# One-core delta-rule attention and routed feed-forward: separate semaphore instructions against counts that ride on the work

## What is computed

```python
# attention: q, k, v, gate, beta by projections of layernorm(x); 16 heads of 32
def step(S, inp):                      # one token, all heads
    k_t, q_t, v_t, beta_t, a_t = inp
    S = S * a_t[..., None, None]
    kv_mem = jnp.einsum('bhd,bhde->bhe', k_t, S)
    delta = (v_t - kv_mem) * beta_t
    S = S + k_t[..., :, None] * delta[..., None, :]
    return S, jnp.einsum('bhd,bhde->bhe', q_t, S)
x = x + layernorm(rmsnorm(ys) * silu(gate) @ Wo.T + bo)
# feed-forward: one of 16 columns per token (top-1 of similarity + sigmoid(gelu gate)),
# y = weight * gelu(x @ W_col + b_col) @ proj + proj_b + x
x = x + layernorm(layernorm(y) * ln_g + ln_b)
```

## Time and profile before

| | us |
|---|---|
| runs (3) | 4015.16, 4022.54, 4012.38 |
| median | 4015.16 |
| profiled execution, its own time | 4013.22 |
| its span, first to last instruction | 4011.4 |
| PE busy, DVE busy | 3183.0, 2954.6 |
| ACT busy, POOL busy | 1356.0, 1903.3 |
| mean granted clock of PE | 0.887 of full |

### The profile page before, as it was taken

The page is one execution under the profiler, slowest core; times in us unless marked ns, Lnnn a source line. Parts: engine busy times, 40 slices in busy tenths (PEclk is TensorE's granted clock), DMA queues, the critical chain, the costliest instruction groups (busy, mean ns, idle before and its releaser), DMA issues. The chain is left out here.

```text
span 4011.4 us, 150558 instructions
## 1 busy us (share of the span) xinstructions
PE 3183.0 (79%) x59368; PEld 2416.1 (60%) x59368; DVE 2954.6 (74%) x12372; ACT 1356.0 (34%) x2440; POOL 1903.3 (47%) x2903
## 2 busy tenths in 40 slices
PE   5788888888888888888888888888888888536664
PEld 4666666666666666666666666666666666424442
DVE  1577877777777777778777777777778777746786
ACT  2233333333333333333333333333333333124553
POOL 0544455444444445444554444544454445414776
PEclk9898999988888898988889988988899889768997
DMA  3654444555544445544455554454555444518995
GB/s 107 119 105 93 97 95 96 103 107 107 97 97 98 95 97 107 107 96 88 93 99 107 107 105 96 96 98 92 104 107 105 94 93 94 104 61 228 231 228 119
DMA packets 400616, 438.62 MB, mean 109 GB/s; under 512 B 34624, under 2 KB 338368, under 8 KB 399440
## 3 DMA queue, kind: packets, MB, share of 16 engines
q1 hardware_dynamic: 383312, 395.67, 47.9%
q0 software_dynamic: 16640, 33.71, 3.8%
HBM read 357.55 MB, written 75.93 MB: 108 GB/s over the span
## 5 line engine op out<-in xcount | busy, mean ns | idle before, releaser
L406 PE MATMUL work<-xT,w_sb 128*128 128x256 f32 x5120 | 1352.6, 416 | 19.1 <-PEq L397 9.5
L1003 POOL TENSOR_TENSOR pairs<-pairs,beta 128x240 f32<-128x240 f32 (+14 forms) x1920 | 851.6, 482 | 891.7 <-POOLq L999 891.7
L406 PEld LDWEIGHTS work<-xT,w_sb 128*128 128x128 f32 x5120 | 1017.9, 206 | 213.0 <-issue 60.3
L1216 DVE TENSOR_TENSOR uk<-uk,Ut 128x120 f32<-128x120 f32 (+14 forms) x3840 | 710.4, 227 | 0.0
L1213 DVE TENSOR_TENSOR Ut<-pairs,uk 128x120 f32<-128x120 f32 (+14 forms) x3840 | 693.9, 218 | 11.4 <-DVEq L1204 6.2
L514 PE MATMUL work<-wo_sb,ctxT 128*128 128x512 f32 x512 | 255.0, 644 | 48.9 <-PEq L397 46.7
L1016 POOL TENSOR_TENSOR kd<-kd,dec 128x512 f32<-128x512 f32 x64 | 68.9, 1076 | 440.0 <-POOLq L1014 434.3
L770 ACT ACTIVATE qraw<-work 128x512 f32<-128x512 f32 x128 | 75.8, 592 | 477.5 <-ACTq L769 477.5
L450 PE MATMUL uk<-kqd,S 32*32 32x32 f32 x8192 | 129.1, 206 | 125.9 <-issue 104.9
L1228 DVE TENSOR_TENSOR S<-Sd,su 128x512 f32<-128x512 f32 x64 | 44.0, 687 | 232.8 <-DVEq L1227 232.8
L1034 POOL TENSOR_TENSOR xfw<-xfw,pb_sb 128x1024 f32<-128x1024 f32 x32 | 75.2, 2351 | 293.7 <-POOLq L1033 293.7
(11 more groups left out here) (211 smaller groups left out, 5872.5 us busy)
## 6 DMA issues: line engine op xcount, KB each, us to landing
pairs<-pair_rows SPq DMA_DIRECT2D x512, 480.0 KB, 8.2
w_sb<-in_w_cols SPq DMA_DIRECT2D x80, 256.0 KB
w_sb<-in_proj_w SPq DMA_DIRECT2D x80, 256.0 KB
pairs<-xs_rows SPq DMA_DIRECT2D x70, 258.0 KB
xt<-in_x SPq DMA_DIRECT2D x66, 256.0 KB
pair_rows<-Ak SPq DMA_DIRECT2D x64, 256.0 KB, 2.6
x<-in_x SPq DMA_DIRECT2D x64, 256.0 KB, 11.7
out<-x SPq DMA_DIRECT2D x64, 256.0 KB, 3.3
```

The source lines that it names most:

```text
L406: mm = pe.matmul(w[:, half * BT:(half + 1) * BT], w_sb[:, f, j * D + hg * P:j * D + (hg + 1) * P], xT[:, f, :], start=(f == 0), stop=(f == ...
L1003: ins = nc.gpsimd.tensor_tensor(a, a, beta[:, :, t:t + WID[t0]], ALU.mult)
L1216: link(v.tensor_tensor(uk[:, g, at + 1:at + 1 + n], uk[:, g, at + 1:at + 1 + n], Ut[:, g, 0:n], ALU.subtract), behind=1)
```

## The change

Signals of the main phase become counts that are never taken down. `Chain.__call__` gets a `signal`: the instruction then raises that signal itself instead of the step semaphore, and the engine does not wait for it unless `hold` says so. `take` waits until a count has reached the sum of all that this reader has taken so far, less `free` for resources that start out free. As nothing is taken down, one count serves several readers: `S_ready` now serves PE and POOL, `kq_ready` PE, POOL and ACT; `kqd_ready`, `A_ready`, `eg_ready`, `xf_ready` also stand for "free" signals that are gone. The bank signals `work_free` are gone too: `into` waits for the count that the bank's last reader raises anyway (`READ_BY`). A wait directly ahead of an instruction rides on it; a second wait for the same instruction is a semaphore instruction of its own. SP's `store` no longer waits for the landing; `load_residual` waits for the store before. The values, shapes and tiles stay.

```diff
+READ_BY = dict(xT="xT_ready", qk="q_sq_ready", ss="ss_read", alpha="alpha_read", rms="rms_read", G="eg_ready", wo="wo_read",
+               rank="rank_read", gate="gate_used", beta="beta_ready", v="v_read", xfT="xfT_ready", hid="h_ready",
+               logits="logits_read")
...
-    def __call__(self, ins, behind=0):
-
+    def __call__(self, ins, signal=None, behind=0, hold=False):
+
+        if signal:
+            self.sent[signal] += 1
+            ins.then_inc(self.s[signal], 1)
+            if hold:
+                self.hold(signal)
+            return
         self.n += 1
         ins.then_inc(self.sem, 1)
         self.eng.wait_ge(self.sem, self.n - behind)
+
+    def hold(self, signal):
+        self.eng.wait_ge(self.s[signal], self.sent[signal])
...
+        seen, sent = Counter(), Counter()
+
+        def take(eng, name, n=1, free=0, use=""):
+
+            seen[eng, name, use] += n
+            if seen[eng, name, use] > free:
+                eng.wait_ge(s[name], seen[eng, name, use] - free)
...
             def load_tokens(i):
-                sp.wait_ge(s["xt_free"], 1)
-                sp.sem_inc(s["xt_free"], -1)
+                take(sp, "eg_ready", 2, free=2)
...
             def load_residual(i):
-                sp.wait_ge(s["x1_free"], 1)
-                sp.sem_inc(s["x1_free"], -1)
+                take(sp, "xf_ready", TB, free=TB)
+                take(sp, "store_done", 16 * BL, free=16 * BL)
...
             def store(i):
...
-                sp.wait_ge(s["store_done"], 16 * BL)
-                sp.sem_inc(s["store_done"], -(16 * BL))
...
             def into(*use):
 
-                pe.wait_ge(bank_free(*use), 1)
-                pe.sem_inc(bank_free(*use), -1)
+                before = holder.get(BANK[use])
+                if before:
+                    pe.wait_ge(s[before[0]], before[1])
+                uses[use[0]] += HID // P if use[0] == "hid" else 1
+                holder[BANK[use]] = READ_BY[use[0]], uses[use[0]]
                 return bank(*use)
...
             def change_state(c, half):
                 if not half:
-                    pe.wait_ge(s["delT_ready"], 1)
-                    pe.sem_inc(s["delT_ready"], -1)
-                    pe.wait_ge(s["kd_ready"], 1)
-                    pe.sem_inc(s["kd_ready"], -1)
+                    take(pe, "delT_ready")
+                    take(pe, "kd_ready")
...
             def copy_and_square(n):
 
-                act.wait_ge(s["qraw_free"], 1)
-                act.sem_inc(s["qraw_free"], -1)
-                act.wait_ge(s["qk_full"], 1)
-                act.sem_inc(s["qk_full"], -1)
-                link(nc.scalar.activation(qraw[n % 2][:], bank("qk", n), ACT.Copy))
-                link(nc.scalar.activation(qsq[n % 2][:], bank("qk", n), ACT.Square))
-                act.sem_inc(bank_free("qk", n), 1)
-                act.sem_inc(s["q_sq_ready"], 1)
+                take(act, "kq_ready", free=2)
+                take(act, "qk_full")
+                nc.scalar.activation(qraw[n % 2][:], bank("qk", n), ACT.Copy)
+                link(nc.scalar.activation(qsq[n % 2][:], bank("qk", n), ACT.Square), "q_sq_ready")
...
             def decay_products(c):
 
-                dve.wait_ge(s["kkq_full"], 1)
-                dve.sem_inc(s["kkq_full"], -1)
+                take(dve, "kkq_full")
                 d = dec[:, :, c * C:(c + 1) * C]
                 link(v.tensor_tensor(Ak[c][:].rearrange("p j g t -> p g j t"),
                                      kkq[:, :, 0, :].rearrange("p g (j t) -> p g j t", j=2),
-                                     d.rearrange("p g (j t) -> p g j t", j=2), ALU.mult))
-                dve.sem_inc(s["Ak_ready"], 1)
-                link(v.tensor_tensor(Aq[c][:], kkq[:, :, 1, :], d, ALU.mult))
-                dve.sem_inc(s["kkq_free"], 1)
-                dve.sem_inc(s["A_ready"], 1)
+                                     d.rearrange("p g (j t) -> p g j t", j=2), ALU.mult), "Ak_ready")
+                link(v.tensor_tensor(Aq[c][:], kkq[:, :, 1, :], d, ALU.mult), "A_ready")
...
-                for g in turns:
-                    link(v.tensor_tensor(uk[:, g, h], uk[:, g, h], beta[:, g, th], ALU.mult), behind=1)
-                dve.wait_ge(s["pr_ready"], 1)
-                dve.sem_inc(s["pr_ready"], -1)
-                if (c, j) == (NC - 1, 1):
-                    dve.wait_ge(dve_step, link.n)
-                    dve.sem_inc(s["vb_free"], 1)
+                for i, g in enumerate(turns):
+                    if i:
+                        take(dve, "pr_ready")
+                    link(v.tensor_tensor(uk[:, g, h], uk[:, g, h], beta[:, g, th], ALU.mult),
+                         "vb_free" if i and (c, j) == (NC - 1, 1) else None, behind=1, hold=True)
...
             def add_to_state():
-                dve.wait_ge(s["su_full"], 1)
-                dve.sem_inc(s["su_full"], -1)
-                dve.wait_ge(s["Sd_ready"], 1)
-                dve.sem_inc(s["Sd_ready"], -1)
-                link(v.tensor_tensor(S[:], Sd[:], su[:], ALU.add))
-                dve.sem_inc(s["S_ready"], 1)
-                dve.sem_inc(s["S_ready_p"], 1)
+                take(dve, "su_full")
+                take(dve, "Sd_ready")
+                link(v.tensor_tensor(S[:], Sd[:], su[:], ALU.add), "S_ready")
```

More of the change, by code:

```diff
@@ L1 @@
 import math
+from collections import Counter
 from contextlib import ExitStack
@@ L330, in store @@
             def store(i):
-                sp.wait_ge(s["x1_ready"], 1)
-                sp.sem_inc(s["x1_ready"], -1)
+                take(sp, "x1_ready", TB)
                 for bl in range(BL):
@@ L437, in key_products @@
                 if not half:
-                    pe.wait_ge(s["kkq_free"], 1)
-                    pe.sem_inc(s["kkq_free"], -1)
+                    take(pe, "A_ready", free=1, use="kkq")
                 on_tiles(half, "kkq_full", lambda g, q, q_half: pe.matmul(
@@ L445, in state_to_u @@
                 if not half:
-                    pe.wait_ge(s["kqd_ready"], 1)
-                    pe.sem_inc(s["kqd_ready"], -1)
-                    pe.wait_ge(s["S_ready"], 1)
-                    pe.sem_inc(s["S_ready"], -1)
+                    take(pe, "kqd_ready")
+                    take(pe, "S_ready")
                 on_tiles(half, "uk_full", lambda g, q, q_half: pe.matmul(
@@ L465, in state_to_outputs @@
                 if not half:
-                    pe.wait_ge(s["uq_free"], 1)
-                    pe.sem_inc(s["uq_free"], -1)
+                    take(pe, "uq_free", free=1)
                 on_tiles(half, None, lambda g, q, q_half: pe.matmul(
@@ L541, in ranks @@
             def ranks():
-                pe.wait_ge(s["oh_ready"], 1)
-                pe.sem_inc(s["oh_ready"], -1)
+                take(pe, "oh_ready")
                 w = into("rank")
@@ L755, in copy_outputs @@
[L755 to L773 removed]
+                take(act, "o_full")
@@ L850, in step @@
                 if after:
-                    act.wait_ge(s["ctx_raw"], 2)
-                    act.sem_inc(s["ctx_raw"], -2)
+                    take(act, "ctx_raw", 2)
                 if ahead:
@@ L980, in _ @@
         def _(pool):
-            link = Chain(pool, pool_step)
+            link = Chain(pool, pool_step, s, sent)
             def decay_state(p, c):
-                pool.wait_ge(s["S_ready_p"], 1)
-                pool.sem_inc(s["S_ready_p"], -1)
+                take(pool, "S_ready")
                 nc.gpsimd.tensor_tensor(Sd[:], S[:], eg_end[p][:, :, c:c + 1].to_broadcast([P, G, DH]), ALU.mult)\
@@ L1214, in solve_half @@
                                              ALU.mult), behind=1)
-                    for g in turns:
+                    for i, g in enumerate(turns):
                         link(v.tensor_tensor(uk[:, g, at + 1:at + 1 + n], uk[:, g, at + 1:at + 1 + n], Ut[:, g, 0:n],
-                                             ALU.subtract), behind=1)
-                dve.wait_ge(dve_step, link.n)
-                dve.sem_inc(pairs_free[j], 1)
-                link(v.transpose(delT[c][:], uk[:]))
-                dve.sem_inc(s["delT_ready"], 1)
@@ L1232, in scale @@
+                link(v.transpose(delT[c][:], uk[:]), "delT_ready")
+            def add_to_state():
+                take(dve, "su_full")
+                take(dve, "Sd_ready")
+                link(v.tensor_tensor(S[:], Sd[:], su[:], ALU.add), "S_ready")
             def scale(n):
                 j, hp = divmod(n, 2)
-                dve.wait_ge(s["q_r_ready"], 1)
-                dve.sem_inc(s["q_r_ready"], -1)
-                link(v.tensor_tensor(unit(kq, hp)[:, :, :, 1 - j, :], per_chunk(qraw[n % 2][:]), per_chunk(qr[n % 2][:]), ALU.mult))
@@ L1238, in scale @@
-                dve.sem_inc(s["qraw_free"], 1)
-                dve.sem_inc(s["kq_ready_pe"], 1)
-                dve.sem_inc(s["kq_ready_p"], 1)
+                take(dve, "q_r_ready")
```

(6 more changed lines are left out.)

398 lines of the change are left out of this document (135 added, 263 removed).

## The result

The changed kernel takes 3640.8 us (median of 4 runs, 3631.2 to 3648.1) where the kernel before takes 4018.9 (4 runs, 4012.4 to 4023.4): ratio 0.9059, 95% interval 0.9028 to 0.9090. That is 378 us less, 9.4%; the forecast was 3815 and the range ended at 3720. The sign was right and the size far too small.

The account below looks back on a forecast made before the run. DVE was taken as the path nearly all the way through a block. Per block 7.5 + 0.3 - 1.2 - 0.4 = 6.2 us, times 32 blocks 198: 4013.2 - 198 = 3815 us; range for 8 in 10: 3720 to 3915.

Parts of the forecast that it names:

- overlap of DVE's neighbours: DVE neighbours that need not wait overlap by 0.1 us at about 15 places per block; up to 1.5, not summed.
- POOL and SP: POOL's 25 dropped instructions and SP's earlier fetch of pairs (0,0) after the store: booked at nothing.
- PE's hand-overs: Release of PE at delT, hidden layer and S: 0.1 us each, 0.3 per block; bounds 0 and 3.8.
- DVE's instructions, less what is waited for: DVE: 79 fewer semaphore instructions per block at 0.105 us, 8.3; less 0.8 before the logits wait, 1.2 and 0.4 booked back.
- ACT: ACT's 84 dropped instructions and its earlier table load before Gelu: counted at zero; the load worth up to 1.3 us.
- What becomes late next: DVE's wait before uk of chunk 1 takes back 1.2 us per block; rank, corr of half 1, alpha and PE halts 0.4.
- They stand in ACT's idle time: ACT's 84 and POOL's 25 dropped instructions count nothing, since their values reach DVE microseconds early; otherwise up to 0.1 us each.
- this is worth nothing: SP fetches pairs (0,0) 3.1 us sooner, but the solve reading them comes after the logits: nothing, range only.
- the rival's floor of 96.1 per block: Rival that PE takes over as bound: 91.3 us busy plus 4.8 of halts per block; 3933 us, chance 0.17.
- more than the sum: Rival: overlaps, PE's 38 instructions and fewer half-speed stretches give 9.2 us per block; 3719 us, chance 0.14.
- That signals cost nothing: Rival: DVE's gaps of 0.15 to 0.44 us are its own drain and stay; 4013 us, chance 0.03.
- PE's matmuls show their weight loads: Rival: a matmul carrying a wait drains PE and shows its 0.206 us weight load, 38 per block; 4064 us, chance 0.03.

Follow-up runs that it names:

- the second signals: All engines' own semaphore instructions put back on the changed kernel, plus DVE's second signal for each second reader, 16 more per block: 4004.2 us, against 3971.5 without these.
- all engines at once: Changed kernel with signals and takes of all engines as own instructions again and SP waiting for the store to land: 3971.5 us, ratio 0.9889.
- the four parts: Changed kernel with own semaphore instructions back on one engine at a time: DVE 3871.8 us, PE 3681.6, ACT 3652.7, POOL and SP with the store wait 3697.8.
- the run with the hold: Changed kernel, but on DVE the instruction after each signalling one waits until that has ended, signals still riding: 3695.4 us, ratio 0.9203.
- the one with kqd put off: Changed kernel with POOL's product kqd of chunk 0 put off until DVE has finished the next tokens' norm: 3595.8 us, ratio 0.8945.
- Putting a part of one back: Changed kernel, but POOL's two products kd wait for both transposes together, as before the change: 3639.1 us, ratio 0.9046.
- the run with PE's instructions put back: Changed kernel with PE alone given back its 38 semaphore instructions per block, 59 against 21: 3681.6 us, ratio 0.9151.

## Why the prediction was wrong

The mechanism was right: DVE is the path nearly all the way, an instruction of its own costs it about 0.1 us, and no long wait swallowed the gain. Three steps of the sum failed: the overlap of DVE's neighbours, measured and then left out (58 us), POOL and SP put at nothing (53 us), and PE's hand-overs put at 10 us (37). Its terms, in us for the whole kernel, beside what the runs give:

| term | booked | measured |
|---|---|---|
| DVE's instructions, less what is waited for | 240 - 51 = 189 | 227 + 32 - 58 = 201 |
| overlap of DVE's neighbours | 0, at most 48 | 58 |
| PE's hand-overs | 10 | 37 |
| POOL and SP | 0 | 53 |
| ACT | 0 | 8 |
| parts beyond their sum, and what wasn't put back | 0 | 9 + 12 |
| sum | 198 | 378 |

The first measured row is worked out, not run: all DVE instructions put back, and the second signals, less the overlap. The 9 us by which all engines at once exceed the sum of the four parts are less than the error of a distance.

- *DVE's instructions.* Confirmed in the net: 79 at 0.105, less 0.8 for those in front of a wait and 1.6 booked back, is 5.9 us per block; 201/35 is 5.7. The gap between Ak and Aq went, as said.
- *The overlap.* This is the largest error by a little, and one of choice: the prediction measured 0.1 per place, bounded it at 1.5 per block, and left it out of the sum and only in a rival. It counted about 15 such places in a block and took 0.1 each; the run with the hold shows 28 at 0.11, 3.1 us in the timeline, of which 1.7 reached the span (58 us). So the forecast "DVE's busy time per block stays at 82 to 83" failed with it: 79.2. What is seen to happen and isn't covered by anything belongs in the sum.
- *What becomes late next.* The size held (1.6 booked), not the place. I had it before uk of chunk 1; there the mean wait per block went from 0.50, most of it DVE's own gap, to 0.19. It came before the correction of half 1 (0.35 to 1.80) and before alpha (0.26 to 0.97).
- *POOL and SP.* "They stand in ACT's idle time" and "this is worth nothing" failed: 26 us for POOL's semaphores, 21 for the store, 53 with SP's own. An engine idle for half of its time can still be the one waited for when it works. Whether a signal is early must be read at each hand-over: for ACT it was, and the zero holds; for POOL's decays it was not. The store was sent off with "the solve that reads those pairs comes after the logits", which looked at the reader and not at POOL's products in between, behind which Sd and kqd wait in POOL's order; that the cost runs over them is likely and not shown.
- *PE.* 0.3 us per block were booked for three hand-overs; 38 instructions cost 37/35 = 1.1. PE's busy time, forecast to stay at 91, fell from 91.4 to 87.7, with the granted clock up from 0.90 to 0.93 of full in the window. Per block the record of the clock has 21.2 us at its lower level (1.2 GHz) before and 15.0 after. So the rival's floor of 96.1 per block was no floor: in the blocks 6 to 28 the changed kernel's block takes 96.3 us, but the one with kqd put off takes 95.1.
- *The calls.* Everything was multiplied by 32. The step is called 35 times, and the partial blocks behind the last transposes got 26 us shorter (from 631.7 to 605.4 us between the last transpose of gT and the end), those before the first 4: 30 of the 382 us between the two profiled spans lie there.
- *DVE's stretched instructions.* 1.6 us per block of DVE's durations went without the change meaning it. Putting a part of one back (0.3 per block) cost nothing that could be measured, taking another away gained 46 us. How much of the 1.6 was on the path of the kernel before stays open; it is contained in the rows of the table above and not a term beside them.

Of the rivals, "more than the sum" (3719, chance 0.14) came nearest, for its first two reasons and with POOL's and SP's share added; the measured 3641 lies beyond it too. That signals cost nothing is excluded by the runs that put them back, and that PE's matmuls show their weight loads by PE's busy time, which fell. PE isn't the bound: DVE's waits on S and the logits are as long as before.

## What to carry to other kernels

Count semaphore instructions of their own per loop on the engine that carries the path, multiply by the gap that the timeline shows (here 0.1 us, of which 0.05 to 0.07 reached the span), and add the overlap of neighbours that need no longer wait for each other, counted place by place (here 28 x 0.11 us, of which half reached the span). Don't book another engine's instructions at nothing because it is often idle: look at each hand-over whether the receiver is already waiting. And before shortening a DVE phase, look for instructions that take ten times their usual length, and which POOL instruction ends with them: moving that one POOL instruction beside work that reads PSUM was worth 46 us here, and cutting it up nothing.

## What was not expected of the hardware

- A DVE instruction of 0.16 us took 2.28 beside a POOL product of 2.34, and 0.65 beside one cut into four, each time until the POOL instruction ended. Cutting also made POOL's product longer, 2.77 us instead of 2.34.
- DVE's neighbours of 0.69 us overlap by 0.08 where neither waits for the other: steps of 0.61 us, 0.72 with a hold between, 0.85 with a signal of its own.
- A semaphore instruction between two DVE instructions that only carries the wait for the first one's end adds nothing (0.03 us of gap with it and without it); one that waits for that end and then raises a signal makes the gap 0.15.
- PE's halts with no wait behind them stay with the change (192 us in the whole trace before, 186 after) and move. Before su they hold 50.0 us before the change and 55.0 in the run with PE's instructions put back, but 9.3 in the changed kernel; before uk it is the other way about. It goes by PE's own program: in the four programs that have PE's semaphore instructions 48 to 60 us stand before su, in the other fourteen 7 to 16. The rows of the changed kernel and then of that run:

```profile
PE uk L460 <- issue: 127.0, 88, 5.7
```

```profile
PE uk L466 <- issue: 67.0, 42, 4.4
...
PE su L493 <- issue: 55.0, 25, 4.9
```

The kept traces also say what these halts wait for. The page of the changed kernel has a DMA queue of instructions:

```profile
q8 instruction: 460, 7.54, 0.9%
```

It has 460 transfers in the fourteen programs without PE's semaphore instructions and 464 in the four with them, whatever the other engines have; so it is PE's. In the trace of the changed kernel PE has 41 halts of over 1.5 us with no wait behind them, 132 us in all, and each ends 1.3 to 1.7 us behind the end of a transfer of that queue; a moment taken at random lies 3.3 us behind one (median; 0.3 to 9.2 for nine in ten). Of the 781 such halts in all eighteen traces 779 end 1.1 to 1.9 us behind one. PE waits there for its next instructions. No run changed the fetching, so what the halts cost in the span isn't known.

The Trainium skill, "Runtime: NRT & Kernel Launch", section "Instruction fetch mechanics", calls the cost of fetching mostly hidden. Here halts of up to 5.7 us aren't.
